# A decoder layer with a mixture of experts: where the experts' output rows wait for the final scatter, and which queues carry the tokens and the results

## The chip, the cores and the metric

One core of one Trainium2 chip runs the whole layer in one launch. The metric is device time in microseconds (us), the median of several executions. Before the change it is 2227.69 us (three runs, 2223.74 to 2231.18).

## The reference, cut to what matters

A pre-norm decoder layer over x of 16 sequences, 224 tokens and 512 features: a low-rank mixer, a cross attention to a context of 750 tokens, and a mixture of 32 experts. The change touches only the end of the third part.

```
x = x + mixer(layernorm(x));  x = x + cross_attention(layernorm(x), ctx)
xn = layernorm(x)
probs = softmax over tokens of (xn @ gate_w.T + gate_b)        # per sequence and expert
vals, idx = the 8 largest of the 224 tokens, for each sequence and expert
merged[b,e] = sum_k vals[b,k,e] * xn[b, idx[b,k,e]]            # one row of 512
h = gelu([merged, 1] @ w1[e]);   o[b,e] = [h, 1] @ w2[e]       # w1: 513x2048, w2: 2049x512
out = x;   out[b, idx[b,k,e]] += vals[b,k,e] * o[b,e]          # scatter
```

Everything is float32. The weights of the 32 experts are 8 MB each, 268 MB in all, and each is used for 16 rows only, one for each sequence.

## The kernel before

The attention parts fill the first 1550 us. While they end, the first weights of the experts are already on their way. Then one block of the program handles the experts, with five instruction streams that meet at semaphores; the order in each is written by hand.

**Weights.** A ring in SBUF has slots of 2 MB (`ring[:, slot, :]`, 128 partitions of 16 KB); four of them hold the weights of an even expert (two for w1, two for w2) and four those of an odd one. SP (SyncE) issues the loads: `load_chunk`, line 457 for w1 and line 463 for w2. A w1 slot is loaded again when the expert before last has gone through its hidden layer (`h_full`), a w2 slot when that expert's output has been multiplied (`o_full`). Behind the four loads of an expert stands the load of its output bias, `b2_row` (line 1576), which waits for `o_out`, the count of finished output rows.

**One expert.** DVE (VectorE) takes the 16 merged rows (`take`), PE (TensorE) multiplies them by w1 (line 1762), ACT (ScalarE) copies the result, PE turns it, DVE adds the bias, ACT applies gelu, PE multiplies by w2 (line 1791) in four column groups, ACT copies these (line 1649), PE sums them with one matmul (`sum_parts`, line 1744), and DVE adds `b2_row` into `o_fin[:, e2, :]` (`row_out`, line 1695): 16 partitions, one for each sequence, 512 numbers; two buffers, for even and odd experts. The sum of an expert is made after the hidden layer of the next, so that only the last one's stands by itself.

**Rows to the scatter.** POOL (GpSimd) issues for each expert but the last one DMA that stores the 16 rows of `o_fin` to `o_rows` in DRAM (line 1624). DVE's `row_out` waits until the rows of all earlier experts are stored. The scatter reads them from `o_in[r*32+e, g, :]`, which holds on partition r*32+e the rows of expert e for the sequences 4g+r. SP brings them there with `read_back`, four DMAs (one for each r) for experts 0 to 15, and four for experts 16 to 30; the last expert's rows go straight from `o_fin` to `o_in` in four small DMAs (line 1614), each onto the partitions 31, 63, 95 and 127.

**Order of SP's queue at the end.** w1 of expert 31; the first four read-backs; four loads of the layer's tokens before the scatter from `out` into ring slots 0 to 3 (line 1606; 2, 2, 2 and 1 MB: 28 tiles of 128 rows by 512, eight tiles to a slot), the first two behind `h_full` of expert 30, the others behind its `o_full`; w2 and `b2_row` of expert 31; the second four read-backs; the last expert's rows.

**Scatter.** For each of 28 tiles PE multiplies `picks` (the weights of the chosen tokens, 32 experts by 128 tokens) by `o_in` (line 1817, one or two matmuls to a tile, each counted twice by the profile), DVE adds the bank to the token tile in the ring (line 1723), and ACT stores the tile to `out` (line 1659), 256 KB each, and waits for all 28 at the end. The tiles of one group g go in the order 0, 2, 4, 6, 1, 3, 5 of seven (`TURN`).

Of the kernel before, what the change touches and what calls it, by code (L numbers as in the profile page):

```python
# [17 lines left out]
F32 = mybir.dt.float32  # L18
# [5 lines left out]
P = 128  # L24
# [54 lines left out]
def build(nc, x, ctx_in, aWq, aWk, aWo, U_b, V_b, W_b, bias_b, U_t, V_t, W_t, X_t, bias_t, alpha,  # L79
          xWq, xWkv, xWo, gate_w, gate_b, w1, w2, out):  # L80
    B, T, D = x.shape
    _, S, DC = ctx_in.shape
    R = V_b.shape[1]
    E, _, H = w1.shape
    NH = 16
    HD = D // NH
# [50 lines left out]
    with es:  # L137
        def sem(name):
            return es.enter_context(nc.semaphore(name))

        def sb(stack, name, shape, dt=F32):
            return stack.enter_context(nc.sbuf_tensor(name, shape, dt))

        bank = [es.enter_context(nc.psum_tensor(f"bank{i}", [P, BANK], F32)) for i in range(8)]
        router = nc.dram_tensor("router", [B, E, T], F32).ap()
        o_rows = nc.dram_tensor("o_rows", [B, E, D], F32).ap()
        routed = nc.dram_tensor("routed", [B, P, KD * E], F32).ap()


# [1360 lines left out]
        o_fin = sb(es, "o_fin", [B, 2, D])  # L1510
        RW = 4
        GB = B // RW
        o_in = sb(es, "o_in", [P, GB, D])
# [14 lines left out]
        o_copied = sem("o_copied")  # L1528
        o_summed = sem("o_summed")
        o_out = sem("o_out")  # L1530
        o_stored = sem("o_stored")
        picks_loaded = sem("picks_loaded")
        o_loaded = sem("o_loaded")
        fin_loaded = [sem(f"fin_loaded{g}") for g in range(GB)]
        scat_begun = sem("scat_begun")
        scat_full = sem("scat_full")
        fin_ready = sem("fin_ready")
        fin_stored = sem("fin_stored")

        NT = B * T // P  # L1540
        PER = 2 * H // D
        rows_out = out.rearrange("b t d -> (b t) d").rearrange("(k p) d -> p k d", p=P)

        def fin(k):

            return ring[:, k // PER, k % PER * D:(k % PER + 1) * D]
# [8 lines left out]
        def tile_at(n):  # L1555

            return n // CYCLE * CYCLE + TURN[n % CYCLE]

        with nc.Block() as block:
            @block.sync  # L1560
            def _(sp):
                def weights(i, e2, first, qs=range(4)):

                    e = i * 2 + e2
                    for q in qs if not first else ():
                        slot = e2 * 4 + q
                        if q < 2:
                            sp.wait_ge(h_full, i * 2 + (e2 - 1))
                        else:
                            sp.wait_ge(o_full, i * 2 + (e2 - 1))  # L1570
                        load_chunk(sp, e, q, slot)
                    if 3 not in qs:
                        return
                    if not first:
                        sp.wait_ge(o_out, i * 2 + (e2 - 1))
                    sp.dma_start(b2_row[:, e2, :],  # L1576
                                 w2[bass.ds(e, 1), H1, :].to_broadcast([B, D])
                                 ).then_inc(b2_loaded[e2], 16)

                weights(0, 0, True)  # L1580
                weights(0, 1, True)
                sp.wait_ge(cleared, 2)
                for r in range(RW):
                    sp.dma_start(picks[r * E:(r + 1) * E, :, LEAD[r]:LEAD[r] + T],
                                 router.rearrange("(g r) e t -> r e g t", r=RW)[r]
                                 ).then_inc(picks_loaded, 16)
                weights(1, 0, False, (1, 2, 3))
                weights(1, 1, False)
                with sp.Fori(2, E // 2 - 1) as i:  # L1589
                    weights(i, 0, False)  # L1590
                    weights(i, 1, False)
                end = E // 2 - 1
                weights(end, 0, False)
                weights(end, 1, False, (0, 1))
                def read_back(r, e0, e1):
                    sp.dma_start(o_in[r * E + e0:r * E + e1, :, :],
                                 o_rows.rearrange("(g r) e n -> r e g n", r=RW)[r, e0:e1, :, :]
                                 ).then_inc(o_loaded, 16)

                sp.wait_ge(o_stored, 16 * (E - 4))  # L1600
                for r in range(RW):
                    read_back(r, 0, E // 2)
                for g in range(-(-NT // PER)):
                    sp.wait_ge(h_full if g < 2 else o_full, E - 1)
                    n = min(PER, NT - g * PER)
                    sp.dma_start(ring[:, g, 0:n * D].rearrange("p (k d) -> p k d", d=D),  # L1606
                                 rows_out[:, g * PER:g * PER + n, :]).then_inc(fin_loaded[g], 16)
                weights(end, 1, False, (2, 3))
                sp.wait_ge(o_stored, 16 * (E - 1))
                for r in range(RW):  # L1610
                    read_back(r, E // 2, E - 1)
                sp.wait_ge(o_out, E)
                for g in range(GB):
                    sp.dma_start(o_in[E - 1:P:E, g, :], o_fin[g * RW:(g + 1) * RW, 1, :]  # L1614
                                 ).then_inc(o_loaded, 16)

            @block.gpsimd
            def _(pool):
                nc.gpsimd.memset(picks[:], 0.0).then_inc(cleared, 1)

                def keep_rows(i, e2):
                    e = i * 2 + e2
                    pool.wait_ge(o_out, i * 2 + (e2 + 1))
                    pool.dma_start(o_rows[:, bass.ds(e, 1), :].rearrange("b o n -> b (o n)"),  # L1624
                                   o_fin[:, e2, :]).then_inc(o_stored, 16)

                with pool.Fori(0, E // 2 - 1) as i:
                    keep_rows(i, 0)
                    keep_rows(i, 1)
                keep_rows(E // 2 - 1, 0)  # L1630
                pool.wait_ge(o_stored, 16 * (E - 1))

            @block.scalar
            def _(act):
                def hidden(i, e2, first):
                    e = i * 2 + e2
                    act.wait_ge(h_full, e + 1)
                    if not first:
                        act.wait_ge(ht_full, e - 1)
                    nc.scalar.copy(hid[:, e2, :], bank[e2][:]).then_inc(h_out, 1)  # L1640
                    act.wait_ge(ht_biased, e + 1)
                    if not first:
                        act.wait_ge(o_full, e - 1)
                    nc.scalar.activation(hid_T[:, e2].rearrange("p t m -> p (t m)"),
                                         bank[2 + e2][:], ACT.Gelu).then_inc(ht_ready, 1)
                    act.wait_ge(o_full, e + 1)
                    if not first:
                        act.wait_ge(o_summed, e - 1)
                    nc.scalar.copy(o_sb[:, e2, :], bank[5 + e2][:]).then_inc(o_copied, 1)  # L1649

                hidden(0, 0, True)
                hidden(0, 1, True)
                with act.Fori(1, E // 2) as i:
                    hidden(i, 0, False)
                    hidden(i, 1, False)
                for n in range(NT):
                    k = tile_at(n)
                    act.wait_ge(fin_ready, n + 1)
                    act.dma_start(rows_out[:, k, :], fin(k)).then_inc(fin_stored, 16)
                act.wait_ge(fin_stored, 16 * NT)  # L1660

            @block.vector
            def _(dve):
# [24 lines left out]
                def row_out(i, e2, first):  # L1688

                    e = i * 2 + e2  # L1690
                    dve.wait_ge(o_summed, e + 1)
                    dve.wait_ge(b2_loaded[e2], i * 16 + 16)
                    if not first:
                        dve.wait_ge(o_stored, e * 16)
                    nc.vector.tensor_tensor(o_fin[:, e2, :], bank[7][0:B, :], b2_row[:, e2, :],  # L1695
                                            ALU.add).then_inc(o_out, 1)

# [21 lines left out]
                for n in range(NT):  # L1719
                    k = tile_at(n)  # L1720
                    dve.wait_ge(fin_loaded[k // PER], 16)
                    dve.wait_ge(scat_full, n + 1)
                    nc.vector.tensor_tensor(fin(k), fin(k), bank[k % 8][:], ALU.add  # L1723
                                            ).then_inc(fin_ready, 1)

            @block.tensor
            def _(pe):
# [76 lines left out]
                sum_parts(E // 2 - 1, 1, False)  # L1804

                pe.wait_ge(picks_loaded, 16 * RW)
                pe.wait_ge(o_loaded, 16 * (2 * RW + GB))

                def scatter(k, r, first, last):

# [51 lines left out]
```

## Time and profile before

| | us |
|---|---|
| median of three runs | 2227.69 (2223.74 to 2231.18) |
| the profiled execution, its own time | 2225.7 |
| its span | 2224.0 |
| experts' block, from the first tokens taken (line 1672) to the end | 1547.9 to 2224.0 |
| the scatter, from its first matmul (line 1817) | 2198.7 to 2224.0 |

The span is the profiler's record of the same execution, 1.7 us shorter than its time. Times in rows are us from the span's start. A DMA has two times: how long its issue held the queue of the engine that issued it, and how long after that it landed. In the view of stretches the last two columns are the mean busy share of the core's 16 DMA engines and what they moved; the share is made of packet times and can come out a little above 1.

### The profile page before, as it was taken

What the parts mean: (1) busy time and instruction counts of PE and PEld (TensorE: products, weight loads), DVE (VectorE), ACT (ScalarE), POOL (GpSimd) and SP (SyncE); (2) the same over time, 40 slices, a digit from 0 to 9 for tenths busy, and PEclk for the clock granted to TensorE, in tenths of its full rate; (3) what the DMA queues carried; (4) which work ended last, traced back from release to release, by engine and by line L of the source; (5) the groups of instructions that cost most, each with busy time, mean ns of one, the idle gap of its engine ahead of it and who ended that gap; (6) DMA issues with size and microseconds to landing.
All of it is one profiled execution on the core that took longest, in us unless ns stands there. A gap on an engine that the chain in (4) does not pass through costs nothing. (4 is left out here: it accounts for less than half of the span.)

```text
span 2224.0 us, 41403 instructions
## 1 busy us (share of the span) xinstructions
PE 1838.5 (83%) x12594; PEld 1205.0 (54%) x12594; DVE 1012.0 (46%) x2542; ACT 746.3 (34%) x1551; POOL 824.1 (37%) x591
## 2 busy tenths in 40 slices
PE   7789999999999999999999999976655556555644
PEld 5667777777777777777777777742211111111111
DVE  1355767657666667676576676642100000000003
ACT  3144445445445454454454544532100000000000
POOL 0255555655555556465655555542000000000000
PEclk9899999999999999999999999977977787778776
DMA  5324333333243243332432433373999999999996
GB/s 170 88 65 105 80 90 93 84 89 89 75 115 78 77 97 84 89 98 75 103 81 77 106 83 74 86 297 125 407 421 422 422 420 423 422 422 419 421 365 241
DMA packets 142370, 421.35 MB, mean 189 GB/s; under 512 B 32140, under 2 KB 78188, under 8 KB 117756
## 3 DMA queue, kind: packets, MB, share of 16 engines
q1 hardware_dynamic: 135580, 411.70, 54.3%
q10 hardware_dynamic: 5760, 8.15, 1.0%
q0 software_dynamic: 992, 1.02, 0.1%
q8 instruction: 21, 0.34, 0.1%
q14 instruction: 17, 0.14, 0.0%
HBM read 307.37 MB, written 17.14 MB: 146 GB/s over the span
## 5 line engine op out<-in xcount | busy, mean ns | idle before, releaser
L1168 DVE TENSOR_REDUCE maxes<-bank 112x1 f32<-112x376 f32 (+1 forms) x1024 | 510.7, 538 | 120.6 <-PE bank L1377 116.8
L970 ACT ACTIVATE probs<-bank 125x448 f32<-125x448 f32 x768 | 399.9, 548 | 149.6 <-PE bank L1399 148.5
L1399 PE MATMUL bank<-q_st,k_st 98*125 98x224 f32 x1536 | 334.6, 304 | 17.6 <-DMA q_st<-max_two 14.7
L848 POOL TENSOR_TENSOR psum_keys<-psum_keys,probs 125x896 f32<-125x896 f32 x127 | 266.9, 2101 | 212.3 <-ACT probs L970 202.9
L1791 PE MATMUL bank<-ring,hid_T 128*32 128x512 f32 x1024 | 177.1, 854 | 203.0 <-DMA ring<-in_L_ffn_w 198.1
L1377 PE MATMUL bank<-k_st,q_st 96*112 96x376 f32 (+1 forms) x1024 | 318.8, 357 | 24.4 <-DVE maxes L1168 20.9
L1399 PEld LDWEIGHTS bank<-q_st,k_st 98*125 98x125 f32 x1536 | 257.0, 190 | 70.9 <-issue 33.5
L1695 DVE TENSOR_TENSOR o_fin<-bank,b_row 16x512 f32<-16x512 f32 x32 | 21.7, 679 | 586.3 <-PE bank L1744 586.3
L851 POOL TENSOR_TENSOR psum_keys<-psum_keys,probs 125x896 f32<-125x896 f32 x127 | 266.9, 2101 | 10.0
L1624 POOL DMA_DIRECT2D o_rows<-o_fin x31 | 15.3, 494 | 596.7 <-DVE o_fin L1695 596.7
L1791 PEld LDWEIGHTS bank<-ring,hid_T 128*32 128x32 f32 x1024 | 44.9, 150 | 311.2 <-issue 305.7
L1377 PEld LDWEIGHTS bank<-k_st,q_st 96*112 96x112 f32 x1024 | 168.5, 179 | 81.1 <-DVE maxes L1168 52.8
L1762 PE MATMUL bank<-ring,tok 128*32 128x512 f32 x1024 | 142.0, 680 | 74.5 <-DMA ring<-in_L_ffn_w 72.4
L844 POOL TENSOR_TENSOR psum_keys<-probs 125x896 f32<-125x896 f32 x64 | 134.2, 2097 | 169.2 <-ACT probs L970 164.7
L1416 PE MATMUL bank<-probs,late 125*32 125x224 f32 x3072 | 187.2, 362 | 0.0
L1649 ACT COPY o_sb<-bank 128x512 f32<-128x512 f32 x32 | 18.7, 586 | 329.1 <-PE bank L1791 329.1
L1762 PEld LDWEIGHTS bank<-ring,tok 128*32 128x32 f32 x1024 | 32.4, 117 | 168.7 <-DMA ring<-in_L_ffn_w 103.1
L808 POOL TENSOR_TENSOR rstd<-mean_var,small 112x2 f32<-112x2 f32 x48 | 9.4, 195 | 307.7 <-DVE mean_var L1049 304.2
L1315 PE MATMUL bank<-yT,wq_T 128*128 128x224 f32 x512 | 110.0, 358 | 4.2 <-DVE k_lo L1113 3.5
L1416 PEld LDWEIGHTS bank<-probs,late 125*32 125x32 f32 x3072 | 80.6, 110 | 57.0 <-issue 20.2
L1341 PE MATMUL bank<-wo_T,o_T 128*112 128x512 f32 x244 | 109.9, 592 | 1.6 <-DVE o_T L1205 1.6
L916 ACT COPY late<-bank 125x512 f32<-125x512 f32 x96 | 56.2, 586 | 153.8 <-PE bank L1334 153.8
(169 smaller groups left out, 2740.4 us busy)
## 6 DMA issues: line engine op xcount, KB each, us to landing
ring<-in_L_ffn_w SPq DMA_DIRECT2D x128, 2048.0 KB, 30.7
k_st<-k_hi SPq DMA_DIRECT2D x512, 93.8 KB, 2.1
k_st<-k_lo SPq DMA_DIRECT2D x256, 93.8 KB, 2.2
q_st<-q_hi SPq DMA_DIRECT2D x504, 28.0 KB, 1.8
ctx_nat<-in_ctx SPq DMA_DIRECT2D x16, 750.0 KB
x_in<-in_x SPq DMA_DIRECT2D x16, 448.0 KB, 3.9
out<-x SPq DMA_DIRECT2D x16, 448.0 KB, 3.1
out<-ring ACTq DMA_DIRECT2D x28, 256.0 KB, 3.0
```

Source lines behind the costliest of these rows:

```text
L844: nc.gpsimd.tensor_tensor(psum_keys[:], lo, hi, ALU.add).then_inc(keys_summed, 1)
L848: nc.gpsimd.tensor_tensor(psum_keys[:], psum_keys[:], lo, ALU.add).then_inc(pool_chain, 1)
L851: nc.gpsimd.tensor_tensor(psum_keys[:], psum_keys[:], hi, ALU.add).then_inc(keys_summed, 1)
L970: nc.scalar.activation(probs[n % 2][:, j, :], bank[5 + u % 2][0:SK, 0:2 * T], ACT.Exp, scale=SCALE).then_inc(probs_ready, 1)
L1168: nc.vector.tensor_reduce(maxes[:, j, t, c:c + 1], score_bank(n)[0:TT, 0:SC[c + 1] - SC[c]], AX.X, ALU.max).then_inc(s_drained, 1)
L1315: last = nc.tensor.matmul(ps[:, 0:T], wq_T[:, kd, i * P:(i + 1) * P], yT[:, kd, :], start=(kd == 0), stop=(kd == KD - 1))
L1341: last = nc.tensor.matmul(ps[0:TT, :], tokens(o_T[:, kt, :], i), wo_T[:, kt, :], start=(kt == 0), stop=(kt == G - 1))
L1377: nc.tensor.matmul(score_bank(n)[0:TT, 0:SC[c + 1] - SC[c]], q_st[slot][0:3 * HD, j, t * TT:(t + 1) * TT], k_st[slot][0:3 * HD, j, chunk(c ...
L1399: last = nc.tensor.matmul(bank[5 + u % 2][0:SK, kk * T:(kk + 1) * T], k_st[slot][:, j, k * SK:(k + 1) * SK], q_st[slot][:, j, :], start=Tr ...
L1416: last = nc.tensor.matmul(bank[7][j * HD:(j + 1) * HD, 0:T], v[:, 2 * c + kk, col:col + HD], p[:, j, kk * T:(kk + 1) * T], start=(c == 0 a ...
L1762: last = nc.tensor.matmul(bank[e2][c * 32:(c + 1) * 32, :], tok[:, e2, kd, :], ring[:, slot, col:col + BANK], start=(kd == 0), stop=(kd == ...
L1791: last = nc.tensor.matmul(bank[5 + e2][c * 32:(c + 1) * 32, :], hid_T[:, e2, t, c * 32:(c + 1) * 32], ring[:, slot, col:col + D], start=(t ...
```

## The change

The DRAM tensor `o_rows` and all eight read-backs go. POOL issues, for every expert but the last, four DMAs from `o_fin` straight into `o_in` (`place_rows`; one for each g, four partitions of 2 KB), written out 31 times instead of in a loop. DVE's `row_out` waits for all of these instead of for the store. The last expert's four DMAs are issued by ACT instead of SP. SP issues all of expert 31's weights and its bias row before the four token loads; the semaphores that the token loads wait for are the same. The 28 stores of tiles are issued by ACT and SP in turn. PE waits for the placements instead of the read-backs.

```
-        o_rows = nc.dram_tensor("o_rows", [B, E, D], F32).ap()
...
+        def place_rows(eng, e, done):
+            for g in range(GB):
+                eng.dma_start(o_in[e:P:E, g, :], o_fin[g * RW:(g + 1) * RW, e % 2, :]
+                              ).then_inc(done, 16)
+
+        def store(eng, n):
+            k = tile_at(n)
+            eng.wait_ge(fin_ready, n + 1)
+            eng.dma_start(rows_out[:, k, :], fin(k)).then_inc(fin_stored[n % 2], 16)
...
                 weights(end, 0, False)
-                weights(end, 1, False, (0, 1))
-                def read_back(r, e0, e1):
-                    sp.dma_start(o_in[r * E + e0:r * E + e1, :, :],
-                                 o_rows.rearrange("(g r) e n -> r e g n", r=RW)[r, e0:e1, :, :]
-                                 ).then_inc(o_loaded, 16)
-
-                sp.wait_ge(o_stored, 16 * (E - 4))
-                for r in range(RW):
-                    read_back(r, 0, E // 2)
+                weights(end, 1, False)
                 for g in range(-(-NT // PER)):
                     sp.wait_ge(h_full if g < 2 else o_full, E - 1)
                     n = min(PER, NT - g * PER)
                     sp.dma_start(ring[:, g, 0:n * D].rearrange("p (k d) -> p k d", d=D),
                                  rows_out[:, g * PER:g * PER + n, :]).then_inc(fin_loaded[g], 16)
-                weights(end, 1, False, (2, 3))
-                sp.wait_ge(o_stored, 16 * (E - 1))
-                for r in range(RW):
-                    read_back(r, E // 2, E - 1)
-                sp.wait_ge(o_out, E)
-                for g in range(GB):
-                    sp.dma_start(o_in[E - 1:P:E, g, :], o_fin[g * RW:(g + 1) * RW, 1, :]
-                                 ).then_inc(o_loaded, 16)
+                for n in range(1, NT, 2):
+                    store(sp, n)
+                sp.wait_ge(fin_stored[1], 16 * (NT // 2))
...
-                with pool.Fori(0, E // 2 - 1) as i:
-                    keep_rows(i, 0)
-                    keep_rows(i, 1)
-                keep_rows(E // 2 - 1, 0)
-                pool.wait_ge(o_stored, 16 * (E - 1))
+                for e in range(E - 1):
+                    pool.wait_ge(o_out, e + 1)
+                    place_rows(pool, e, o_placed)
...
-                for n in range(NT):
-                    k = tile_at(n)
-                    act.wait_ge(fin_ready, n + 1)
-                    act.dma_start(rows_out[:, k, :], fin(k)).then_inc(fin_stored, 16)
-                act.wait_ge(fin_stored, 16 * NT)
+                act.wait_ge(o_out, E)
+                place_rows(act, E - 1, last_placed)
+                for n in range(0, NT, 2):
+                    store(act, n)
+                act.wait_ge(fin_stored[0], 16 * (NT // 2))
...
-                        dve.wait_ge(o_stored, e * 16)
+                        dve.wait_ge(o_placed, e * 16 * GB)
...
-                pe.wait_ge(o_loaded, 16 * (2 * RW + GB))
+                pe.wait_ge(o_placed, 16 * GB * (E - 1))
+                pe.wait_ge(last_placed, 16 * GB)
```

## Rows read from the trace of the kernel before

**Rows 1.** the page: busy shares, and the DMA row of its 40 slices
```profile
PE 1838.5 (83%) x12594; PEld 1205.0 (54%) x12594; DVE 1012.0 (46%) x2542; ACT 746.3 (34%) x1551; POOL 824.1 (37%) x591
...
DMA  5324333333243243332432433373999999999996
```

**Rows 2.** the chain of waits, 2120 to 2224: start us, us, what (q: a queue)
```profile
2132.03 18.59 SPq L1606
...
2150.66 7.54 SPq L1606
...
2158.24 5.38 SPq L1606
...
2166.27 20.98 DMA ring<-in_L_ffn_w
...
2187.39 5.22 PE bank L1791 x32
...
2196.80 1.77 DMA o_in<-o_fin
...
2198.71 9.01 PE bank L1817 x39
```

**Rows 3.** DMA by queue (packets, MB, share) and one issue, 1610 to 2120
```profile
q1 hardware_dynamic: 21941, 213.93, 100.6%
q0 software_dynamic: 832, 0.85, 0.5%
...
o_rows<-o_fin POOLq DMA_DIRECT2D x25, 32.0 KB, 5.6
```

**Rows 4.** stretches: window, us, busy us of each engine, granted PE clock, DMA share, GB/s
```profile
1610.00:2110.00 500.00, 290.03 (x1740) 81.52 (x1744) 39.78 (x144) 43.19 (x74) 11.69 (x24) 0.78 1.01 421
2128.00:2144.00 16.00, 10.25 (x54) 2.95 (x58) 1.60 (x6) 1.18 (x2) 0.48 (x1) 0.68 1.02 424
2144.00:2154.00 10.00, 2.13 (x20) 0.45 (x15) 0.00 (x0) 0.59 (x1) 0.00 (x0) 0.78 1.02 172
2154.00:2170.00 16.00, 6.11 (x22) 1.61 (x22) 1.57 (x5) 1.18 (x2) 0.48 (x1) 0.61 1.04 374
...
2180.00:2188.00 8.00, 0.61 (x4) 0.23 (x8) 0.00 (x0) 0.00 (x0) 0.00 (x0) 0.50 0.62 151
2204.00:2220.00 16.00, 11.93 (x61) 5.56 (x56) 14.82 (x25) 0.00 (x0) 0.00 (x0) 0.93 0.99 378
```

**Rows 5.** timeline of the queues: start us, us, engine, line, operation
```profile
2114.96 10.38 SPq L1596 DMA_DIRECT2D o_in<-o_rows  x4
...
2134.49 0.48 POOL L1624 DMA_DIRECT2D o_rows<-o_fin  x1 [19.74 <-DVE o_fin L1695]
...
2168.14 2.76 SPq L1596 DMA_DIRECT2D o_in<-o_rows  x4
...
2201.57 19.68 ACTq L1659 DMA_DIRECT2D out<-ring  x28
```

**Rows 6.** timeline of PE and DVE, 2111 to 2224
```profile
2118.65 5.41 PE L1791 MATMUL bank<-ring,hid_T 128*32 128x512 f32 x32 [5.29 <-DMA ring<-in_L_ffn_w]
...
2133.17 0.68 DVE L1695 TENSOR_TENSOR o_fin<-bank,b_row 16x512 f32<-16x512 f32 x1 [18.55 <-PE bank L1744]
...
2138.88 5.53 PE L1791 MATMUL bank<-ring,hid_T 128*32 128x512 f32 x32 [5.28 <-DMA ring<-in_L_ffn_w]
...
2159.70 0.68 DVE L1695 TENSOR_TENSOR o_fin<-bank,b_row 16x512 f32<-16x512 f32 x1 [24.93 <-PE bank L1744]
...
2194.35 0.68 DVE L1695 TENSOR_TENSOR o_fin<-bank,b_row 16x512 f32<-16x512 f32 x1 [33.08 <-PE bank L1744]
...
2202.59 16.23 DVE L1723 TENSOR_TENSOR ring<-ring,bank 128x512 f32<-128x512 f32 x27 [1.05 <-PE bank L1817]
```

**Rows 7.** the page, stores of the tiles: engine queue, count, KB each, median us to landing
```profile
out<-ring ACTq DMA_DIRECT2D x28, 256.0 KB, 3.0
```

**Rows 8.** landing of the 31 row stores, in the view of tile o_rows
```profile
DMA to landing us min/median/max: 4.8/5.6/6.1
```

More of the change, by code:

```diff
@@ L1530, in build @@
         o_out = sem("o_out")
-        o_stored = sem("o_stored")
+        o_placed = sem("o_placed")
+        last_placed = sem("last_placed")
         picks_loaded = sem("picks_loaded")
-        o_loaded = sem("o_loaded")
         fin_loaded = [sem(f"fin_loaded{g}") for g in range(GB)]
@@ L1537, in build @@
         fin_ready = sem("fin_ready")
-        fin_stored = sem("fin_stored")
+        fin_stored = [sem(f"fin_stored{i}") for i in range(2)]
         NT = B * T // P
@@ L1619, in _ @@
                 nc.gpsimd.memset(picks[:], 0.0).then_inc(cleared, 1)
[L1621 to L1625, printed above, removed]
-                with pool.Fori(0, E // 2 - 1) as i:
-                    keep_rows(i, 0)
-                    keep_rows(i, 1)
-                keep_rows(E // 2 - 1, 0)
-                pool.wait_ge(o_stored, 16 * (E - 1))
+                for e in range(E - 1):
+                    pool.wait_ge(o_out, e + 1)
+                    place_rows(pool, e, o_placed)
             @block.scalar
```

## The prediction

> **What bounds the kernel now.** I read the page's busy shares first. PE is busy 83% of the span, but the DMA row shows nines in the last third [rows 1], and the change lies there. The DMA view of the steady part of the experts' block settles it: the SP queue alone fills 100.6% of the 16 engines, POOL's stores 0.5% [rows 3]. The reader is to see that neither PE nor DVE sets the pace: PE's w2 matmuls start 20.23 us apart (2118.65, 2138.88), and each waited 5.3 us for its weights [rows 6].
>
> The chain of waits shows where the pattern breaks. The second token load holds SP's queue for 18.59 us, the third for 7.54, the fourth begins at 2158.24, and behind them stand expert 31's w2 loads, which land only 20.98 us after the issue of the last; PE begins at 2187.39 [rows 2]. From there all is serial: w2 matmuls, copy, sum, `o_fin` at 2194.35 [rows 6], four small DMAs, the scatter from 2198.71 [rows 2], stores until 2221.25 [rows 5], the end at 2224.0. So 25.3 us of scatter and 11.3 us before it follow the last weights.
>
> The view of stretches shows what stands ahead of these weights. From 2128 to 2144 the DMA engines move 424 GB/s. From 2144 to 2154 they are just as busy (1.02) but move 172; from 2154 to 2170 it is 374; from 2180 to 2188 151, at a share of 0.62 [rows 4]. The slow stretch is where the first read-backs (issued 2114.96 to 2125.34) come through the queue, the second where those issued at 2168.14 do [rows 5]. The 374 belongs to the tokens, moved in rows of 2 KB instead of 8 or 16.
>
> **The weights come first.** By the period, expert 31's w2 matmuls would begin at 2138.88 + 20.23 = 2159.1 with nothing ahead of the weights, not at 2187.39: 28.3 us earlier. The parts agree. Tokens, 7.34 MB at 374 GB/s: 19.6 us. First read-backs, 0.52 MB at 424: 1.2 us, and the stretch's loss, 10 us less 1.72 MB at 424 (4.1): 5.9 us. That makes 26.7, and leaves 1.6 for the second read-backs, which overtake the last weights in part. The tokens' cost is only moved; that of the read-backs goes. What is late next: the hidden layer of expert 31 (its `o_fin` of expert 30 came at 2133.17 + 20.2 in rhythm, gelu some 2 us behind), 3 to 4 us before the weights; it doesn't decide.
>
> Of SP's queue every issue counts: w2 of expert 31 now waits for `o_full` 30, which came at about 2124.1 (2118.65 + 5.41 [rows 6]); its bias row waits for `o_out` 30, at 2133.9. The tokens stand behind that wait, issued from 2134 instead of 2131.6. By then two w1 and two w2 loads, some 20 us of transfer, are queued, so nothing runs dry. The queue accepts the later loads only as room comes; SP has no other work until the first odd store, at about 2178, and the loads are all accepted well before that (the fourth took 5.4 us after the third [rows 2]).
>
> **Placements in the loop.** 31 single stores of 32 KB become 124 DMAs of 8 KB. The bytes and the 16 packets of 2 KB per expert stay; the target is SBUF, where weights are being written. No row shows SBUF-to-SBUF packets beside the weights; the bias rows, 32 KB an expert from DRAM into 16 partitions, come nearest, and with them the engines hold 421 GB/s over 500 us [rows 4]. From below: nothing, as the stores now (0.5% of the engines [rows 3]). From above by the read-backs, the only small rows written into `o_in`: 256 packets cost 5.9 us, 0.023 us each; 31 x 16 = 496 packets would cost 11.4 us. An expert's 16 packets are spread over 20 us and over four DMAs, not crowded like the read-backs, so I stay near the stores: +2 us, ends 0 and 11.4.
>
> POOL has 4 issues of 0.48 us [rows 5] and landing of 4.8 to 6.1 us [rows 8]: 2 to 8 us in a period of 20, hidden. At the end the cover is thin: rows of expert 30 are ready at 2154.1 + 2, issued by 2158.5, landed by 2164.6; DVE's `row_out` of expert 31, behind which only the scatter's adds are queued, wants them at 2159.1 + 2 + 7.0 (2194.35 - 2187.39) = 2168.1. If a placement takes POOL over 0.9 us more than an issue does now, this begins to cost. Also 0 here, ends 0 and 4.
>
> **The last rows, by ACT.** Now `o_fin` begins at 2194.35 and the scatter at 2198.71: 4.4 us, of which 1.77 is the landing in empty queues [rows 2]. Issued by ACT it is the same four DMAs, but with tokens on all engines. A store lands in 3.0 us in full queues [rows 7], so +1 us; ends 0 and 4. ACT has nothing else to do then; its first store stands behind them and needs them anyway.
>
> **Scatter and stores.** Scatter from 2168.1 + 4.4 + 1 = 2173.5, the first add 2 us later. Tiles need slot 0 at once, slot 1 from the 9th, slot 2 from the 16th, slot 3 from the 26th; at DVE's 0.60 us a tile (16.23 / 27 [rows 6]) that is 2175.5, 2180.3, 2184.5, 2190.5. The tokens follow the last weights (2161.1) at 5.6 us per 2 MB: 2166.7, 2172.3, 2177.9, 2180.7. At least 6.6 us of cover, so DVE won't wait, but the stores now meet the tokens' tail.
>
> Stores from one queue take ACT 19.68 / 28 = 0.70 us each [rows 5], DVE finishes at 2218.8 and ACT at 2221.25, 2.4 us later. But the DMA engines are 0.99 busy at 378 GB/s [rows 4], so 7.34 MB need 19.4 us whoever issues. The Trainium skill, "DMA: Bandwidth & Descriptors", section "Issuing engines are not separate DMA queues", says a second issuing engine saves only issue time; the trace agrees where it shows 0.99. By that rule the second queue is worth nothing here; by ACT's lag alone it would be worth up to 2.4 us. I take 0.5 us, ends -1 (two queues in each other's way) and 2.4.
>
> Two sums then. The chain: 2224.0 - 28.3 + 2 + 1 - 0.5 = 2198.2. The transfers: tokens in at 2180.7, stores 19.4 us behind them if they get no share before: 2200.1. The end is the later of two that lie 2 us apart and share some work; I take a span of 2199.5. Outside the span lie 1.7 us (2225.7 - 2224.0), so 2201.2 in the terms of the profiled execution, which is 2.0 us under the median of the runs shown, inside their spread of 7.4. With half of that: 2202 us, 25.7 under 2227.69. A measurement of this kernel can tell about 0.3% (6.7 us) from no change.
>
> **The rivals.**
> A, placements hold up the weights. Four rows of an expert go onto four partitions that the weights also fill. For it: the stretch at 172 GB/s with busy engines, a sign that small writes into few partitions hold up large ones. Against: there 256 packets came at once. Price 11.4 us in place of 2: 2211. The Trainium skill, "SBUF — State Buffer", section "Door 1: The DMA port swizzle", lets partitions p and p+32 share a port of some 27 GB/s; an expert's placements then put 16 KB on each of two ports. An estimate from that page's figures is 0.6 us on these two, 18.7 us in all if every expert waited for it (2219), 2.4 us if the deep queues even it out; no row shows placements.
> B, the last placements or expert 30's come late because the queues are full of token rows: the scatter starts when the tokens are in, 2180.7 less the 1 us of its start, and not at 2173.5. 2180 + 25.3 = 2205.3, time 2208 on the same basis. For it: a row store lands in 5.6 us, not 1.8. Against: it was so under weights of 8 and 16 KB as well, and ACT has a queue of its own.
> C, more gained: placements free (-2), stores paced by DVE (-2.4 in all): chain 2224.0 - 28.3 + 1 - 2.4 = 2194.3, if the stores share the engines with the tokens' tail well: 2197. Against: the store stretch is full already.
> D, slower: each placement packet stalls not one engine but the whole stream, because it writes a port that the ring's large packets hold. At 0.088 us a packet (2 KB at 374 GB/s over 16 engines), 16 packets cost 1.4 us an expert, 43.6 in all: 2202 - 2 + 43.6 = 2244. It turns the sign above 28/31 = 0.9 us an expert. Against: the bias rows, 32 KB written to SBUF for every expert in the same rhythm, leave the engines at 421 GB/s [rows 4].
> E, the tokens' order does nothing, because the scatter has to wait for their last slot: the cover above of 6.6 us must be lost first. It would need tokens at half their rate; the end then comes 19.6 us after the 2200.1 of the transfers, at 2220, with what lies around it 2222.
>
> **How the numbers follow.** Forecast 66% (2202, own range 2195 to 2208), A 13%, B 10%, C 7%, D 3%, E 1%. The range 2194 to 2212 holds the forecast, B, C and somewhat over half of A. Faster by over 0.3% means under 2221: all but D, E and the tail of A: 0.95; within 0.3% 0.02; slower 0.03.
>
> **What would show it.** Right: PE's last line 1791 starts at 2159 to 2162; no stretch under 350 GB/s before it; steady period 20.2 to 20.3 us; scatter from 2172 to 2175; DVE without a wait for a token slot; the last stores landing at 2198 to 2201. Wrong: a period of 20.6 or more (A, D), a wait of the last `row_out` on POOL or over 3 us to land the last rows (B), DVE waiting for the ring (E), or DMA engines idle in the store stretch.

## The result, and the profile after

The changed kernel takes 2212.18 us (median of six runs, 2208.36 to 2213.57) where the kernel before takes 2229.24 (six runs on the same chip): a ratio of 0.9927, 95% interval 0.9909 to 0.9945. It is 17.1 us faster; 25.7 were forecast, and the time lies 0.2 us above the stated range. The profiled execution has a span of 2209.9 us, 14.1 under that of before.

The chain of waits of the changed kernel (start us, us, what), from the issue of expert 31's last weights to the scatter. It answers to [rows 2]:

```profile
2134.70 34.40 DMA ring<-in_L_ffn_w
...
2169.24 5.89 PE bank L1779 x32
...
2176.87 0.69 DVE o_fin L1683
...
2177.58 0.60 ACTq L1560
...
2179.30 5.13 DMA o_in<-o_fin
...
2184.57 9.02 PE bank L1806 x38
```

The three token loads that held SP's queue are gone from the chain; between the last issue and the w2 matmuls stands one transfer. These matmuls start at 2169.24 instead of 2187.39: 18.1 us earlier, not 28.3. And the last rows take 5.13 us to land, not 1.77: from the w2 matmuls to the scatter's first it is 15.3 us instead of 11.3, 3.4 of these 4.0 in the landing. The scatter starts 14.1 us earlier, and all of that reaches the end.

The timeline of SP, ACT, PE and DVE at the end of the changed kernel, against [rows 5, 6]:

```profile
2128.46 5.76 PE L1779 MATMUL bank<-ring,hid_T 128*32 128x512 f32 x32 [5.65 <-DMA ring<-in_L_ffn_w]
...
2142.28 33.84 SPq L1607 DMA_DIRECT2D ring<-out  x4
...
2148.80 5.82 PE L1779 MATMUL bank<-ring,hid_T 128*32 128x512 f32 x32 [7.16 <-DMA ring<-in_L_ffn_w]
...
2187.44 17.17 ACTq L1566 DMA_DIRECT2D out<-ring  x14
2188.46 16.23 DVE L1711 TENSOR_TENSOR ring<-ring,bank 128x512 f32<-128x512 f32 x27 [1.06 <-PE bank L1806]
2189.18 16.00 SPq L1566 DMA_DIRECT2D out<-ring  x14
```

The stretches of the changed kernel (window, us, busy us of each engine, granted PE clock, DMA share, GB/s), against [rows 4]:

```profile
1610.00:2110.00 500.00, 285.60 (x1702) 80.63 (x1700) 41.23 (x150) 43.61 (x74) 55.99 (x100) 0.76 1.01 415
2144.00:2154.00 10.00, 5.20 (x28) 1.52 (x32) 0.00 (x0) 0.00 (x0) 0.42 (x1) 0.66 1.02 412
2154.00:2170.00 16.00, 6.54 (x50) 1.96 (x46) 1.48 (x5) 1.77 (x3) 2.24 (x4) 0.90 1.01 399
2170.00:2180.00 10.00, 6.13 (x34) 1.42 (x26) 0.68 (x1) 0.58 (x1) 0.00 (x0) 0.81 1.05 387
2180.00:2188.00 8.00, 3.43 (x16) 2.26 (x19) 0.69 (x1) 0.00 (x0) 0.00 (x0) 0.54 0.78 277
2188.00:2204.00 16.00, 13.80 (x68) 7.01 (x62) 15.54 (x26) 0.00 (x0) 0.00 (x0) 0.91 0.93 348
```

The stretch at 172 GB/s is gone, as forecast: 412 and 399 stand in its place. But read the first line. Over 500 us of steady work the engines move 415 GB/s, not 421, at the same full share of 1.01. That is 1.4% less; over 28 experts of some 20 us it comes to some 8 us, the larger part of what is missing. The DMA view of this stretch, against [rows 3], and the landings of the 124 placements, against [rows 8]:

```profile
q1 hardware_dynamic: 21262, 206.90, 100.4%
q0 software_dynamic: 3157, 0.82, 0.8%
...
o_in<-o_fin POOLq DMA_DIRECT2D x100, 8.0 KB, 6.5
```

```profile
DMA to landing us min/median/max: 5.1/6.4/8.5
```

The bytes of queue 0 are as before (0.82 MB). Its packets are not: 3157 against 832. (A packet is a piece of a transfer that one engine moves.) That is 32 packets for every DMA that POOL issues, whether it moves 16 rows (832 for 26) or four. In the trace an expert's packets are 16 rows of 2 KB and, besides, 16 of 4 bytes before and 112 of 4 bytes now.

Two measures are used below. The **period** is the mean distance of the starts of `o_fin`'s additions (line 1695 before) from expert 4 to 29, 25 periods. The **block** is the time from the first of these additions to the end of the span. The block leaves out the attention part, whose length differs from execution to execution: the first addition begins anywhere from 1561.2 to 1571.9 us in these twelve profiles, and at 1567.7 in the changed kernel against 1565.4 before.

### The profile page after: what moved, and what is told of

Read it like the earlier page. It is cut to its first block and busy times, and to the rows that moved or that the text cites. A ratio compares the mean times of both kernels' runs of the same rounds, so it can differ in the third digit from the quotient of the medians.

```text
span 2209.9 us, 41365 instructions
## 1 busy us (share of the span) xinstructions
PE 1841.2 (83%) x12594; PEld 1208.2 (55%) x12594; DVE 1012.3 (46%) x2542; ACT 746.4 (34%) x1551; POOL 879.0 (40%) x684
## 5 line engine op out<-in xcount | busy, mean ns | idle before, releaser
L1779 PE MATMUL bank<-ring,hid_T 128*32 128x512 f32 x1024 | 183.5, 882 | 196.6 <-DMA ring<-in_L_ffn_w 191.6
L1376 PE MATMUL bank<-k_st,q_st 96*112 96x376 f32 (+1 forms) x1024 | 319.5, 358 | 21.8 <-DVE maxes L1167 18.7
L1560 POOL DMA_DIRECT2D o_in<-o_fin x124 | 69.6, 564 | 544.9 <-DVE o_fin L1683 544.9
L1750 PE MATMUL bank<-ring,tok 128*32 128x512 f32 x1024 | 136.1, 655 | 62.7 <-DMA ring<-in_L_ffn_w 60.6
L1637 ACT COPY o_sb<-bank 128x512 f32<-128x512 f32 x32 | 18.7, 586 | 329.0 <-PE bank L1779 329.0
```

Source lines behind the costliest of these rows:

```text
L1376: nc.tensor.matmul(score_bank(n)[0:TT, 0:SC[c + 1] - SC[c]], q_st[slot][0:3 * HD, j, t * TT:(t + 1) * TT], k_st[slot][0:3 * HD, j, chunk(c ...
L1750: last = nc.tensor.matmul(bank[e2][c * 32:(c + 1) * 32, :], tok[:, e2, kd, :], ring[:, slot, col:col + BANK], start=(kd == 0), stop=(kd == ...
L1779: last = nc.tensor.matmul(bank[5 + e2][c * 32:(c + 1) * 32, :], hid_T[:, e2, t, c * 32:(c + 1) * 32], ring[:, slot, col:col + D], start=(t ...
```

## The experiments

| kernel | median us | ratio to before (95%) | period us | block us |
|---|---|---|---|---|
| before | 2229.24 | | 20.18 | 658.6 |
| changed | 2212.18 | 0.9927 (0.9909 to 0.9945) | 20.36 | 642.2 |
| order alone | 2216.01 | 0.9955 (0.9942 to 0.9969) | 20.12 | 648.0 |
| placements alone | 2224.46 | 0.9995 (0.9985 to 1.0004) | 20.38 | 656.8 |
| changed, one store queue | 2210.80 | 0.9929 (0.9912 to 0.9947) | 20.35 | 643.6 |
| before, four stores an expert | 2235.44 | 1.0046 (1.0030 to 1.0062) | 20.46 | 667.5 |
| before, eight stores an expert | 2246.42 | 1.0080 (1.0057 to 1.0103) | 20.74 | 677.8 |
| changed, ACT places | 2217.25 | 0.9954 (0.9942 to 0.9967) | 20.61 | 646.1 |
| changed, tokens held | 2214.53 | 0.9950 (0.9934 to 0.9967) | 20.37 | 643.8 |
| one wide read-back | 2202.52 | 0.9889 (0.9868 to 0.9910) | 20.07 | 633.6 |
| changed, again | 2209.99 | 0.9927 (0.9910 to 0.9945) | 20.35 | 644.0 |
| one wide read-back, again | 2201.60 | 0.9895 (0.9877 to 0.9913) | 20.14 | 633.9 |

Each ratio is to runs of the kernel before on the same chip, whose medians were 2229.24, 2226.11, 2227.11 and 2225.85 in the four sessions.

### Order alone

```
-                weights(end, 1, False, (0, 1))
+                weights(end, 1, False)
...
-                weights(end, 1, False, (2, 3))
```

> The kernel before with one part of the change: SP issues all of expert 31's weights before the first read-backs' neighbours, that is ahead of the tokens; read-backs, DRAM rows and the one store queue stay as they were. Main theory: the tokens' and read-backs' time is only moved behind the weights. Expert 31's w2 matmuls start at about 2160 instead of 2187, or at 2164 to 2166 if the first read-backs, which stand right behind its weights, hold them up in part; but the second read-backs now stand behind 7.3 MB of tokens and land only near 2190, so the scatter starts at 2191 to 2194 instead of 2198.7: 5 to 7 us gained, 2223 us against 2229. Period of the experts unchanged at 20.13 us. Rival (the order is worth its whole 28 us by itself): 2203. Rival (the slow stretch of 172 GB/s belongs to the tokens' first rows and not to the read-backs): the stretch appears behind the first token load.

It gained 10.1 us, more than expected, from the order alone, with a period of 20.12. The timeline of the queues and PE:

```profile
2132.06 5.01 SPq L1596 DMA_DIRECT2D o_in<-o_rows  x4
...
2138.40 6.09 PE L1790 MATMUL bank<-ring,hid_T 128*32 128x512 f32 x32 [6.98 <-DMA ring<-in_L_ffn_w]
...
2162.76 5.86 PE L1790 MATMUL bank<-ring,hid_T 128*32 128x512 f32 x32 [11.13 <-DMA ring<-in_L_ffn_w]
...
2172.36 3.96 SPq L1596 DMA_DIRECT2D o_in<-o_rows  x4
...
2187.30 17.37 PE L1816 MATMUL bank<-o_in,picks 32*128 32x512 f32 x80 [16.93 <-DMA o_in<-o_fin]
```

Expert 31's w2 matmuls start 24.4 us after expert 30's. The first read-backs, which now stand behind the weights, still hold them up by 4 us, and the stretches show the slow one at their place, 2150 to 2160, with the tokens behind it:

```profile
2140.00:2150.00 10.00, 8.02 (x61) 2.16 (x54) 0.00 (x0) 0.59 (x1) 0.00 (x0) 0.83 0.99 416
2150.00:2160.00 10.00, 1.63 (x10) 0.60 (x5) 1.48 (x5) 1.18 (x2) 0.49 (x1) 0.68 1.03 279
2160.00:2170.00 10.00, 6.54 (x34) 1.62 (x34) 0.00 (x0) 0.59 (x1) 0.00 (x0) 0.64 1.04 335
```

The second read-backs and last rows landed at 2187.2, sooner than I had reckoned (2190). The rival of 28 us by order alone is out, and so is the one that puts the slow stretch down to the tokens. The last rows, issued by SP behind its own tokens, took 9.06 us to land:

```profile
2178.10 9.06 DMA o_in<-o_fin
```

### Placements alone

```
-                    pool.dma_start(o_rows[:, bass.ds(e, 1), :].rearrange("b o n -> b (o n)"),
-                                   o_fin[:, e2, :]).then_inc(o_stored, 16)
+                for e in range(E - 1):
+                    pool.wait_ge(o_out, e + 1)
+                    place_rows(pool, e, o_stored)
...
-                for r in range(RW):
-                    read_back(r, 0, E // 2)
...
-                    read_back(r, E // 2, E - 1)
```

> The kernel before with one other part of the change: POOL places each expert's rows straight into the scatter's operand by four DMAs, no DRAM rows and no read-backs; the tokens stay ahead of the last w2 weights, stores from one queue, the last rows issued by SP. Main theory: the period grows from 20.13 to 20.39 us as in the changed kernel (+7.2 us over 28 experts), the read-backs' 8.7 us go, and the last rows land in empty queues in 1.8 us: 2224 to 2229, about 1.5 us under the kernel before. Rival (the longer period comes from something else of the change, or of that run): period 20.13, 2220. Rival (a late landing of the last rows comes from the placements and not from the tokens): landing 5 us here too.

As expected: a period of 20.38 and nothing that can be told from no change. What the read-backs cost at the end, the placements cost in the loop. The stream, too, moves 416 GB/s over 1610 to 2110, as in the changed kernel. In the chain of waits the last rows land in 1.77 us, as before:

```profile
2195.13 1.77 DMA o_in<-o_fin
```

So the late landing does not belong to the placements. Here SP issued these rows, as before, and the tokens were in already; whether the tokens' new place or ACT's issue makes them late is told apart by Tokens held back.

### One store queue

```
-                for n in range(1, NT, 2):
-                    store(sp, n)
...
-                for n in range(0, NT, 2):
+                for n in range(NT):
                     store(act, n)
```

> The changed kernel with all 28 stores issued by ACT, as before. Main theory: the DMA engines are full in the store stretch, whoever issues, so the scatter takes 25.3 us from its first matmul to the end and the time is that of the changed kernel, 2212 within 1 us. Rival (the second queue hides ACT's lag): 2 to 2.4 us slower, 2214.5.

```profile
2180.98 17.20 PE L1804 MATMUL bank<-o_in,picks 32*128 32x512 f32 x80 [7.69 <-DMA o_in<-o_fin]
...
2183.84 19.53 ACTq L1566 DMA_DIRECT2D out<-ring  x28
```

From the first matmul of the scatter to the end 25.2 us (2180.98 to 2206.2), against 25.3 with two queues. The second queue is worth nothing that these runs can show.

### Four stores and eight stores

```
-                    pool.dma_start(o_rows[:, bass.ds(e, 1), :].rearrange("b o n -> b (o n)"),
-                                   o_fin[:, e2, :]).then_inc(o_stored, 16)
+                    for g in range(GB):
+                        pool.dma_start(o_rows[g * RW:(g + 1) * RW, bass.ds(e, 1), :
+                                              ].rearrange("b o n -> b (o n)"),
+                                       o_fin[g * RW:(g + 1) * RW, e2, :]).then_inc(o_stored, 16)
```

(and the same with eight parts of two rows; the waits count accordingly)

> The kernel before with each row store to DRAM cut into four DMAs of four rows by POOL: as many DMAs and completions as the direct placements have, the same bytes, but no write into SBUF. It tells apart why the period grew. Theory a (number of DMAs and their completions): period 20.3 to 20.4 us instead of 20.13, time 2234 to 2236. Theory b (writes into partitions that the weights are filling): period 20.13 to 20.18, time 2229 to 2230.

> The kernel before with each row store to DRAM cut into eight DMAs of two rows by POOL. Four gave a period of 20.46 us (0.28 to 0.33 over the kernel before). If the cost goes with the number of DMAs, 7/3 of that: a period of 20.8 to 20.9, 2246 us. If it was the step from 16 rows on 16 engines to 4 rows on 4 engines, it stays near 20.5, 2236.

The stretches and the queues over the same 500 us, four stores first:

```profile
1610.00:2110.00 500.00, 302.05 (x1728) 81.47 (x1728) 39.61 (x144) 43.01 (x73) 49.77 (x96) 0.77 1.01 421
...
q1 hardware_dynamic: 21492, 209.68, 100.4%
q0 software_dynamic: 3200, 0.83, 0.7%
...
o_rows<-o_fin POOLq DMA_DIRECT2D x96, 8.0 KB, 6.2
```

```profile
1610.00:2110.00 500.00, 288.90 (x1681) 79.73 (x1680) 40.93 (x150) 43.02 (x73) 100.99 (x195) 0.79 1.01 419
...
q0 software_dynamic: 6144, 0.81, 1.1%
...
o_rows<-o_fin POOLq DMA_DIRECT2D x195, 4.0 KB, 6.0
```

No row is written to SBUF here, and yet the period is as long as with the placements, 20.46 us against 20.36. With eight it is 20.74. The bytes are the same, the packets go with the number of DMAs: 3200 for 100, 6144 for about 195, 32 for each. Against 20.07 to 20.18 with one DMA an expert (four profiles) the period is 20.35 to 20.38 with four placements (five profiles). From the middle of the first, some 20.15, three DMAs more cost 0.2 (placements) to 0.3 us an expert and seven more about 0.6: 0.07 to 0.10 us for each.

But the two do not cost it in the same way. With four placements the stream itself is slower, 415 or 416 GB/s in all five profiles. With four stores to DRAM, just as many DMAs and packets, it stays at the 421 of before (one profile; 419 in the one with eight), and the period grows all the same. To see where the time goes, I counted in the trace, packet by packet, how many MB of weights had been moved at the start of each expert's w2 matmuls beyond the load that these had waited for. At expert 5 it is 1.0 to 1.2 MB in every kernel. At expert 29 it is 1.1 to 1.4 MB with one DMA an expert, 1.2 to 1.7 with four placements by POOL, but 3.9 with four stores and 6.7 with eight. These 2.9 and 5.6 MB more are 6.8 and 13.3 us of the stream over 24 experts, 0.28 and 0.55 us each: nearly the whole of what the period has grown by. So with the stores the bytes flow as fast, and the loads are complete later and later behind them. My reading is that some of the 16 engines fall behind while the others run ahead; the trace does not say which engine moved a packet.

For the placements it is the other way round: 1.3% less rate is 0.26 us of a period, all of the growth. The same four DMAs an expert with the other target do not slow the rate, so the write into SBUF does come into it; how it does, these runs do not show.

### ACT places the rows

```
+                    if e:
+                        act.wait_ge(o_out, e)
+                        place_rows(act, e - 1, o_placed)
...
-                for e in range(E - 1):
-                    pool.wait_ge(o_out, e + 1)
-                    place_rows(pool, e, o_placed)
```

> The changed kernel with the placements of experts 0 to 30 issued by ACT (behind its gelu of the next expert, its stream written out instead of looped) and none by POOL. Same rows, same targets, same number of DMAs, another way of issuing them. Theory a1 (what costs 0.25 us an expert is how POOL's DMAs are made up: in the changed kernel's window of 500 us its queue has 3157 packets for 100 DMAs, of which 400 are rows): the period falls back from 20.36 to about 20.15 us, 2206 us. Theory a2 (any four DMAs instead of one cost it, or rows written to SBUF on few engines): period 20.35 or more, 2212 or above.

It is worse: 20.61 us. ACT's queue shows only 8 packets a DMA, four rows and four completions:

```profile
q10 hardware_dynamic: 768, 0.79, 0.5%
```

So fewer packets didn't help. The stream moves 418 GB/s here, and the count of above stands at 5.0 MB at expert 29: 0.38 us an expert of the growth is again loads that are complete late.

The Trainium skill, "DMA: Bandwidth & Descriptors", section "Why a DMA increments its semaphore by 16 and not by 1", says that a DMA issued this way with four partitions runs on the lowest four of the engines; 16 rows of 0.088 us (2 KB at 374 GB/s over 16 engines, as in the prediction) then put 0.35 us on each of these four instead of 0.09, and the weights wait for the slowest. That estimate, 0.26 us more than one store, explains somewhat over half of the 0.45 measured. The 5.0 MB agree with engines that have fallen behind; that it is these four no view here shows, and the rest stays open.

### Tokens held back

```
                     sp.wait_ge(h_full if g < 2 else o_full, E - 1)
+                    if g == 2:
+                        sp.wait_ge(last_placed, 16 * GB)
```

> The changed kernel with one wait more: SP issues the third and fourth token load only when the last expert's rows are placed. It tells why these take 5.1 us to land instead of 1.8. If they stand behind rows of tokens that the DMA engines already hold: with two loads nearly done by then they land in 1.8 to 2.5 us and the scatter starts 3 us earlier after expert 31's w2 matmuls (12 instead of 15.3 us); the DMA engines idle some 5 us before, and the end stays within 2 us of 2212. If the late landing is due to ACT's queue or to the number of DMAs, it stays at 5 us and the time rises to 2215 or more.

The last rows land in 1.78 us:

```profile
2180.66 1.78 DMA o_in<-o_fin
```

The scatter starts 11.9 us after the w2 matmuls (2170.70 to 2182.58) instead of 15.3. ACT issued them here as in the changed kernel. So rows of tokens on the DMA engines are what they waited behind, not ACT's queue. But the engines idle meanwhile, and the held tokens meet the stores: the scatter to the end takes 30.1 us instead of 25.3, and nothing is won (2214.53 against 2212.18). The stretches show the idling, shares of 0.80 and 0.57 where the changed kernel has 1.05 and 0.70:

```profile
2170.00:2180.00 10.00, 6.78 (x34) 1.56 (x34) 0.68 (x1) 0.58 (x1) 0.00 (x0) 0.75 0.80 297
2180.00:2190.00 10.00, 7.42 (x31) 4.55 (x32) 4.22 (x7) 0.00 (x0) 0.00 (x0) 0.66 0.57 190
```

### One wide read-back

```
+                for e in range(E - 2):
+                    pool.wait_ge(o_out, e + 1)
+                    for at in ([e, E - 2, E - 1] if e == 0 else [e]):
+                        pool.dma_start(o_rows[:, at, :], o_fin[:, e % 2, :]
+                                       ).then_inc(o_stored, 16)
+                pool.wait_ge(o_out, E - 1)
+                pool.wait_ge(o_loaded, 16)
+                place_rows(pool, E - 2, o_placed)
...
                 weights(end, 1, False)
+                sp.wait_ge(o_stored, 16 * E)
+                sp.dma_start(o_in[:], o_rows.rearrange("(g r) e n -> (r e) g n", r=RW)
+                             ).then_inc(o_loaded, 16)
```

> A version that keeps the order of the change but not its placements: POOL stores the rows of experts 0 to 29 to DRAM with one DMA each as before; SP reads them back behind the last weights in a single DMA of 128 partitions and 1 MB (two filler rows of each sequence are overwritten later); experts 30 and 31 are placed directly behind it, by POOL and ACT; DVE waits for the stores. If the period is set by the number of DMAs: 20.13 us, expert 31's w2 matmuls at 2161 or so. The scatter then waits for expert 30's placement, issued behind the read-back (near 2167) and landing 6 us later, and starts at 2175 to 2178 instead of 2184.6: 2203 to 2206 us. If narrow read-backs (16 partitions) were slow because of their few partitions, the single one takes under 4 us and no stretch falls below 350 GB/s; if reading rows of 2 KB from this DRAM tensor was slow in itself, there is such a stretch again, some 10 to 20 us of it, and the gain is lost.

> The changed kernel itself, again, to stand beside the version with one wide read-back on the same chip. Theory: period 20.36 us, last rows landing in 5.1 us, 2211 us, 15 to 17 us under the kernel before.

> The version with one store an expert and one wide read-back, again, on the same chip as the changed kernel. Theory: period 20.1 us, 2203 us, 7 to 9 us under the changed kernel, of which 28 x 0.25 = 7 us from the period and the rest from read-back and placements beside the last weights. If its first result was the luck of few runs, it lies within 3 us of the changed kernel.

It beats both kernels: 2202.52 and, again, 2201.60 us. Side by side on one chip it is 8.4 us under the changed kernel (2209.99), and the slowest of its runs (2204.24) lies under the fastest of the other (2208.82). The timeline, the stretches and the DMA view of its end:

```profile
2141.63 0.37 SPq L1608 DMA_DIRECT2D o_in<-o_rows  x1
...
2162.70 5.00 PE L1791 MATMUL bank<-ring,hid_T 128*32 128x512 f32 x32 [7.02 <-DMA ring<-in_L_ffn_w]
...
2165.84 2.27 POOL L1563 DMA_DIRECT2D o_in<-o_fin  x4 [29.31 <-DMA o_in<-o_rows]
...
2170.20 2.23 ACTq L1563 DMA_DIRECT2D o_in<-o_fin  x4
...
2177.22 17.37 PE L1818 MATMUL bank<-o_in,picks 32*128 32x512 f32 x80 [7.77 <-DMA o_in<-o_fin]
```

```profile
1610.00:2110.00 500.00, 296.78 (x1750) 82.97 (x1750) 41.53 (x150) 44.19 (x75) 12.11 (x25) 0.78 1.01 421
...
2150.00:2160.00 10.00, 4.20 (x30) 1.20 (x22) 1.48 (x5) 1.18 (x2) 0.00 (x0) 0.93 1.00 407
2160.00:2165.00 5.00, 2.30 (x12) 0.69 (x16) 0.00 (x0) 0.00 (x0) 0.00 (x0) 0.50 1.04 387
```

```profile
o_in<-o_rows SPq DMA_DIRECT2D x1, 1024.0 KB, 23.7
```

The period is that of before (421 GB/s). One megabyte comes back in a single DMA over 128 partitions, landing 23.7 us after its issue, which is the queue ahead of it, and no stretch near it is slow: 407 and 387 GB/s, where narrow read-backs of half the size had 279 in the order alone and 172 before [rows 4]. So their slowness goes with their shape, four DMAs of 16 partitions each in place of one of 128, and not with the rows' place in DRAM; whether the partitions or the number of DMAs makes it was not tested. The scatter starts at 2177.22 with tokens still behind it, and in the second profile at 2169.69, where the block had begun 8.4 us earlier:

```profile
2164.43 5.13 DMA o_in<-o_fin
...
2169.69 9.02 PE bank L1818 x38
```

## Why the prediction was wrong

**The weights come first: right in kind.** 28.3 us were to be gained before the last w2 matmuls. 18.1 came. Three things make up the difference of 10.1: the block began 2.3 us later, in a part that the change does not touch; experts 0 to 2 lost another 0.6; and 28 periods from expert 3 to 31 lost 7.2 (w2 matmuls at 1598.23 and 2169.24 against 1595.26 and, in rhythm, 2159.1). That is the next point. No stretch under 350 GB/s was left before these matmuls, as forecast.

**Placements in the loop: the step that failed.** I put +2 us, near the lower end, because "The bytes and the 16 packets of 2 KB per expert stay". I counted what the DMAs move and not the DMAs. My own rows had it otherwise: [rows 3] has 32 packets for each DMA, 16 of them rows, so four DMAs leave 128 and not 16. And I leaned on the bias rows of [rows 4], one load an expert from DRAM, which say nothing of four DMAs more out of SBUF. The placements cost 7.2 us between these two profiles, 0.26 an expert (5 to 9 us over 28 experts by the spread of the periods), and as a slower stream: 415 GB/s against 421. Placements alone shows the same without the rest of the change, and one wide read-back, without placements in the loop, is back at 421.

My upper end of 11.4 held it, but came from the read-backs, which are another transfer. Rival A, placements that hold up the weights, came nearer in size (11.4) and in kind: the stream is slower with placements and not with as many stores to DRAM. Its price was no better founded than my upper end. By the port rule of the Trainium skill, "SBUF — State Buffer", section "Door 1: The DMA port swizzle", it came out, as estimates from that page's figures, at 2.4 or 18.7 us; the 7.2 measured agree with neither, and no run here shows ports. That stores to DRAM lengthen the period as well, by loads that are complete late, stood in neither. Rival D, the side that would have made it slower, needed 0.9 us an expert; it is out. What in the writes to SBUF slows the stream stays open.

**The last rows: mis-sized.** +1 us was put, 3.4 came (5.13 against 1.77 and the same four issues), inside the ends of 0 and 4 and over the 3 us that were named as a sign of rival B. Tokens held shows that the tokens do it. Rival B had the scatter wait for all of the tokens, some 7 us; it is about half. The median landing of a tile's store, 3.0 us, was the wrong row to take it from: these are large stores behind each other, not small rows behind token loads. The w2 matmuls of expert 31 took 0.7 us longer, too (5.89 against 5.22).

**Expert 30's placement: right.** Issued from 2162.5 to 2164.7 and landed within 8.5, nothing waited for it: DVE added expert 31's rows 0.02 us behind PE's sum.

**Scatter and stores: right, but for the half us.** 25.3 us before and after, though the scatter began at 2184.57 and not from 2172 to 2175. The second queue was put at 0.5 and is nothing; the row of 0.99 busy engines said so, and so did the Trainium skill, "DMA: Bandwidth & Descriptors", section "Issuing engines are not separate DMA queues". With that and with placements that are not free rival C is out; and as DVE never waited for a token slot, so is E.

**The sum.** 2224.0 - 28.3 + 2.3 + 0.6 + 7.2 + 4.0 = 2209.8, against 2209.9. The 4.0 are the last rows and w2 matmuls. Without the 2.3 us that are not the change's the gain is 16.4, near the 17.1 of the medians.

## What to carry to other kernels

When one DMA is cut into several, count the DMAs, not only the bytes: beside a saturated weight stream each extra small DMA from POOL lengthened the period by 0.07 to 0.10 us, every time, whether its rows went to SBUF or to DRAM. A busy share of 1.01 and an unchanged rate do not show that the loads are complete in time: look at the period of the engine that waits for them. One version moved the small results once, over all 128 partitions, behind the last load that matters, and only the two experts that were too late for it directly; it was the fastest. What must land behind a transfer that was moved away from the front can be late because of it: look at who still has to land while it runs.

## What the runs showed of the hardware

POOL's DMAs of 2 to 16 rows each leave 32 packets in queue 0. Four placements into SBUF an expert bring the stream from 421 to 415 GB/s; four stores to DRAM leave it at 421, and yet its loads are complete later by 0.28 us an expert, eight by 0.55. The same four placements through ACT leave 8 packets each and cost more, 0.45 us an expert instead of 0.2. Small transfers issued by ACT land in 1.8 us when the tokens are held back, and in 5.1 to 5.3 behind rows of 2 KB queued by SP, though they have a queue of their own; issued by SP behind these rows they took 9.1. Four DMAs of 2 KB rows into 16 partitions each brought everything in flight down to 172 GB/s over 10 us (279 where the weights stood ahead of the tokens), where one DMA of rows of the same size into 128 partitions left it at 387 or more in its first profile and at 369 or more, over 5 us at a time, in its second.
